# Ranks of the edges made in four blocks of columns, three of them during the scatter, and 14 turns of first gathers in place of 20

## The chip, the cores and the metric

The kernel is one program on one core of a Trainium2 chip. The metric is the device time of one execution in microseconds (us); lower is better. The engines are TensorE (PE, with its weight loads as PEld), VectorE (DVE), ScalarE (ACT), GpSimd (POOL) and SyncE (SP).

## The reference

Two graph layers over N = 6250 nodes of D = 256 features and E = 106250 edges, sorted by destination. Cut to what matters:

```python
h = (x - mean) * rsqrt(var + EPS) * gamma + beta            # statistics over the nodes
feat_in, feat_out = h @ W_in + b_in, h @ W_out + b_out
a_in  = segment_sum(feat_in[src]  * iw[:, None], dst, N)     # sum at the sorted end
a_out = segment_sum(feat_out[dst] * ow[:, None], src, N)     # sum at the unsorted end
xi, hh = concat(a_in, a_out) @ W_x2i + b_x2i, h @ W_h2h
x1 = layernorm(x + gates(xi, hh, h))
f  = (x1 - mean(x1)) / (std(x1) + 1e-4)
out = layernorm(x1 + segment_sum(iw[:, None] * f[src], dst, N) @ weight + bias)
```

## The kernel before

The edges stand in 208 groups of 512 (4 columns of 128; `CPG = 4`), and four groups are a turn (`RING = 4` buffers of gathered rows in `big`). POOL's program is a row of indirect DMAs, four to a group, each of 128 rows:

* **First gathers** (L541), groups 0 to 79: `FIRST = 20` turns. Rows x[src] come in; ACT scales them (`in_scale`, L665), DVE makes a one-hot matrix of the destinations (`hot_in`, L1518), PE multiplies (`in_mm`, L952), and DVE adds the product into `in_sums` (`add_in`, L1533). A gather of group g waits until `in_mm` of group g - 4 is done.
* **Scatter** (L547), all 208 groups in 52 turns: rows x[dst] are loaded as one block and spread by a one-hot product (DVE L1758, PE `out_mm` L1072), scaled by ACT (`out_messages`, L729) and written by an indirect DMA to slots of the table `messages`, so that the messages of one source tile stand together. Beside it DVE sums the weights (L1761, L1771, L1775, `add_weights` L1750) and once a turn helps with the tile's hidden rows (L1792, L1793, L1797).
* **Rest of the first gathers** (L541), groups 80 to 207 in 32 turns, with `back_mm`: the 232 pairs of message blocks are read back (SP, 260 KB a block), multiplied by one-hots (PE L1140) and added (DVE L1891). `pairs_of(g)` spreads the 232 pairs evenly over those groups, 1.81 to a group: one or two.
* The gates of the first layer, then the **second gathers** (L619), 208 groups, from the table of the first layer's result.

The slot of a message is its rank among the edges of its tile plus the tile's base. DVE makes the ranks during the first gathers. `rank_steps(k)` takes two of the 50 tiles at once (k and k + 25, packed in one number) over all 832 columns: compare, running sum, read the count (L1577), pick, add. There are 25 such k. The counts give the bases (`tile_bases` and what follows it). `base_steps(k)` then adds the bases, three instructions over 832 columns for each of 25 k (L1593 to L1595), in turns 14 to 18. `main_slots` turns ranks into slots: 16 columns before the scatter, the other 816 behind its first turn.

In the same turns x's statistics are made: 24 loads of 256 KB (`x_load`, two tiles of rows each, called a pair; four buffers `xs`) for the sums (PE L965, one pair a group, turns 1 to 6), and the same 24 again for the squares (DVE `x_shift` L1471, ACT `x_square` L660, PE L970, turns 7 to 13). Turns 14 to 19 prepare the weights.

`in_order` deals a list of steps out to the four groups of a turn, a run of consecutive steps to each. In `in_turn` one step stands between `hot_in(g)` and `add_in(g - 1)`, the others behind `add_in`. Every engine works in its program's order; semaphores join them.

Of the kernel before, what the change touches and what calls it, by code (L numbers as in the profile page):

```python
# [4 lines left out]
P = 128  # L5
# [20 lines left out]
FIRST = 20  # L26
# [55 lines left out]
def gnn_program(nc, x, src, dst, edge_weight, edge_weight_n2, gamma, beta, w_in, b_in, w_out, b_out,  # L82
                w_x2i, b_x2i, w_h2h, w_l1, b_l1, out):
    ctx = ExitStack()
    with ctx:
# [49 lines left out]
        win, mask, scan, rank, half_win, half_unit, upper_half, win_b = (part_c(k) for k in range(8))  # L135
        mask_i, scan_i = mask.bitcast(I32), scan.bitcast(I32)
        win_m, scan_m, rank_m, half_win_m, upper_m = (v[:, 0:NM] for v in (win, scan, rank, half_win, upper_half))
        mask_im, scan_im = mask_i[:, 0:NM], scan_i[:, 0:NM]
# [130 lines left out]
        unit, picked = banks23[:, 0:NM], banks67[:, 0:NM]  # L269
        numbers_in, numbers_out = banks67[:, NM:NM + P], ps[6][:, D + P:2 * D]  # L270
# [18 lines left out]
        RANKED = 14  # L289
        CLEARED = 2 * NTP // 5  # L290
        BASES_T = 5
# [9 lines left out]
        X_SHIFT = 1 + XPAIRS // RING  # L301
        PREP = RANKED
        BATCHES = -(-NT // RING)
        TURN_LAG, WEIGH_LAG, FINAL_LAG = 2, 3, 4

# [319 lines left out]
        def _(act):  # L625
# [59 lines left out]
            for i in range(X_SHIFT, X_SHIFT + XPAIRS // RING):  # L685
                for s in range(RING):
                    in_scale(i, s)
                    x_square(RING * (i - X_SHIFT) + s, s)
            x_square(XPAIRS, 0, TAIL, 1)
            scale_turn(X_SHIFT + XPAIRS // RING)  # L690
# [200 lines left out]
        def _(pe):  # L891
# [70 lines left out]
            def x_sum(i, s):  # L962

                pe.wait_ge(S[f"xs_loaded{s}"], 16 * i)
                nc.tensor.matmul(ps[0][:, :], ones[:, :], xs[:, s, :], start=isinstance(i, int) and i == 1 and s == 0, stop=False).then_inc(S["x_used"], 1)  # L965

            def x_square_sum(i, s):

                pe.wait_ge(S["x_sq"], RING * (i - X_SHIFT) + s - 1)
                nc.tensor.matmul(ps[1][:, :], ones[:, :], xs[:, (s - 2) % RING, :], start=isinstance(i, int) and i == X_SHIFT and s == 2,  # L970
                                 stop=False).then_inc(S["x_sq_used"], 1)

            def first_square_sums(i, s):
                if s >= 2:
                    x_square_sum(i, s)

            def last_square_sums(i, s):
                if s < 2:
                    x_square_sum(i, s)
                elif s == 2:  # L980
# [5 lines left out]
            for i in range(2, 1 + XPAIRS // RING):  # L986
                in_turn(i, x_sum)
# [121 lines left out]
            pe.wait_ge(S["base_chain"], 3 * PACKED + 1)  # L1109
# [170 lines left out]
        def _(dve):  # L1280
# [173 lines left out]
            V.memset(rank_m, 0.0)  # L1454
            link(V.tensor_scalar(upper_m, win_m, float(PACKED), None, ALU.is_ge))
            link(V.scalar_tensor_tensor(half_win_m, upper_m, -float(PACKED), win_m, ALU.mult, ALU.add))
            V.tensor_copy(numbers_in, iota[:, :])
            link(V.tensor_scalar(unit, upper_m, 4095.0, 1.0, ALU.mult, ALU.add))
# [6 lines left out]
            def x_shift(i, s):  # L1465

                def run():
                    dve.wait_ge(S[f"xs_loaded{s}"], 16 * (i - X_SHIFT + XPAIRS // RING + 1))
                    mean = mean_b[:, :].rearrange("p (o d) -> p o d", o=1).broadcast_to([P, 2, D])
                    v = xs[:, s, :].rearrange("p (t d) -> p t d", t=2)  # L1470
# [97 lines left out]
            def rank_steps(k):  # L1568

                def step(n, do):  # L1570
                    def run():
                        dve.wait_ge(S["rank_chain"], k * 5 + n + 1)
                        do().then_inc(S["rank_chain"], 1)
                    return run

                def pick():
                    V.tensor_scalar(cnt[:, bass.ds(k, 1)], picked[:, NM - 1:NM], rest_cnt[:, bass.ds(k, 1)], None, ALU.add).then_inc(S["rank_chain"], 1)  # L1577
                    dve.wait_ge(S["rank_chain"], k * 5 + 4)
                    return V.scalar_tensor_tensor(picked, half_win_m, iota_w[:, bass.ds(k, 1)], picked, ALU.is_equal, ALU.mult)
# [689 lines left out]
```

## Time and profile before

| | us |
|---|---|
| median of 3 runs | 3980.32 |
| lowest and highest | 3976.53, 3981.31 |
| the profiled execution's own time | 3986.79 |
| its span in the trace | 3985.0 |
| first gathers, groups 0 to 79 (first gather issued to first scatter issued) | 19.7 to 484.7 |
| scatter | 484.7 to 1736.2 |
| rest of the first gathers (first and last issue) | 1736.2 to 2520.7 |
| second gathers (first and last issue) | 2740.7 to 3946.9 |

The span runs from the first to the last instruction of the core. Busy time is that of each engine, PE's with modelled ends; the idle time before a group of instructions is put down to what seems to have ended it ("remote" is an event whose owner the trace does not know, "issue" is time of the engine's own sequencer).

### The profile page before, as it was taken

To read this page: it belongs to the slowest core of one execution; us is meant where nothing else is said; L and a number is where in the kernel's file an instruction comes from. 1 tells how busy PE (TensorE), PEld (TensorE's weight loads), DVE (VectorE), ACT (ScalarE), POOL (GpSimd) and SP (SyncE) were. 2 spreads that over 40 slices of the span, in tenths; PEclk is the share of its full clock that TensorE was granted. 3 is DMA by queue.
4 is the path that set the end of the run, shared out by engine and by line. 5 is a ranking of instruction groups with operands and counts; after the bars stand their busy time and mean duration, and the time that the engine had idled before them with its cause. 6 is when DMAs were issued, how large, how long until landed. Compare 5 with 4: busy or idle time off the path is not lost.

```text
span 3985.0 us, 48703 instructions
## 1 busy us (share of the span) xinstructions
PE 2654.7 (67%) x10701; PEld 1911.2 (48%) x10701; DVE 2213.6 (56%) x5022; ACT 1059.6 (27%) x3137; POOL 2560.1 (64%) x2706
## 2 busy tenths in 40 slices
PE   4665665665656565658888888995656555555467
PEld 3544533333333333337777777642434444434355
DVE  6866866655566655645565566684233333434244
ACT  3243332222222222234444444562000000000012
POOL 5666666666666666666666666576666666666653
PEclk8787887777877877779999999997777776677789
DMA  5443343333343433357877778554333333333333
GB/s 148 139 131 105 95 139 134 131 131 129 134 136 131 135 132 130 128 156 243 247 246 244 244 242 246 185 164 135 88 91 92 92 91 94 90 91 93 91 108 95
DMA packets 275048, 565.36 MB, mean 142 GB/s; under 512 B 55583, under 2 KB 121110, under 8 KB 274771
## 3 DMA queue, kind: packets, MB, share of 16 engines
q0 software_dynamic: 119808, 329.02, 26.5%
q1 hardware_dynamic: 146304, 223.88, 18.4%
q10 hardware_dynamic: 8660, 9.41, 0.7%
q8 instruction: 96, 1.57, 0.2%
q14 instruction: 180, 1.47, 0.1%
HBM read 419.19 MB, written 142.88 MB: 141 GB/s over the span
## 4 chain that ended last, share of the span: by engine, by line
PE 37%; another core or an unknown queue 22%; issue 17%; DVE 12%; POOL 5%; ACT 2%; SPq 2%; DMA 1%; DVEq 1%; ACTq 0%; POOLq 0%
PE ps L1140 10%; PE ps L952 9%; PE ps L1211 7%; POOL messages L547 4%; PE ps L1072 3%; DVE arena L1758 2%; PE ps L1173 1%; PE ps L1101 1%; ACT arena L729 1%; DVE arena L1761 1%; SPq L498 1%; PE ps L1258 1%; DVE arena L1771 1%; DVE ps L1582 1%
## 5 line engine op out<-in xcount | busy, mean ns | idle before, releaser
L547 POOL DMA_INDIRECT messages<-arena x832 | 825.8, 993 | 429.6 <-issue 243.7
L541 POOL DMA_INDIRECT arena<-in_x,arena x832 | 789.5, 949 | 473.4 <-issue 207.3
L619 POOL DMA_INDIRECT arena<-x_table,wh x832 | 801.4, 963 | 416.5 <-issue 238.4
L1211 PE MATMUL ps<-arena 128*128 x2048 | 624.4, 460 | 383.0 <-SPq L495 165.6
L1211 PEld LDWEIGHTS ps<-arena 128*128 128x128 f32 x2048 | 459.4, 232 | 550.4 <-issue 481.5
L952 PE MATMUL ps<-arena 128*128 128x128 f32 x3328 | 487.2, 308 | 245.8 <-issue 168.2
L952 PEld LDWEIGHTS ps<-arena 128*128 128x128 f32 x3328 | 457.5, 219 | 326.0 <-issue 283.3
L729 ACT ACTIVATE arena<-ps,arena 128x256 f32<-128x256 f32 x832 | 324.1, 480 | 901.3 <-remote 488.5
L2171 DVE TENSOR_TENSOR node_a<-node_a,ps 128x256 f32 x256 | 106.6, 417 | 746.4 <-remote 554.2
L1072 PE MATMUL ps<-arena 128*128 128x256 f32 x1664 | 481.0, 441 | 12.9 <-issue 7.4
L1072 PEld LDWEIGHTS ps<-arena 128*128 128x128 f32 x1664 | 374.6, 227 | 101.4 <-issue 40.1
L665 ACT ACTIVATE arena<-arena 128x256 f32<-128x256 f32 x832 | 352.0, 494 | 185.9 <-DMA arena<-in_x,arena 171.2
L1775 DVE TENSOR_REDUCE arena<-arena 128x128 f32<-128x512 f32 x208 | 214.8, 1033 | 193.6 <-remote 155.0
L2162 DVE TENSOR_SCALAR arena<-iota,arena 128x128 f32<-128x128 f32 x1024 | 291.6, 359 | 0.0
L1758 DVE TENSOR_SCALAR arena<-ps,pcol 128x512 f32<-128x512 f32 x208 | 154.4, 742 | 185.2 <-remote 177.1
L1891 DVE TENSOR_TENSOR node_c<-node_c,ps 128x258 f32 x464 | 195.3, 421 | 111.3 <-issue 72.4
L1140 PE MATMUL ps<-arena 128*128 128x258 f32 x928 | 224.4, 390 | 31.1 <-issue 30.8
L1061 PE MATMUL ps<-w,b_b 128*128 128x512 bf16 x208 | 93.6, 450 | 211.4 <-DVE arena L1758 154.8
L1140 PE MATMUL ps<-arena,bias_b 128*128 128x258 f32 x928 | 223.2, 389 | 15.7 <-issue 12.7
L1533 DVE TENSOR_TENSOR node_a<-node_a,ps 128x256 f32 x208 | 87.4, 420 | 259.4 <-remote 168.0
L872 ACT ACTIVATE arena<-ps 128x256 f32<-128x256 f32 x49 | 18.6, 383 | 762.0 <-PE ps L1249 662.5
L767 ACT ACTIVATE wh<-arena 128x2 f32 x464 | 94.9, 205 | 409.7 <-issue 267.1
(279 smaller groups left out, 3175.3 us busy)
## 6 DMA issues: line engine op xcount, KB each, us to landing
arena<-messages SPq DMA_DIRECT2D x464, 260.0 KB
arena<-in_x SPq DMA_DIRECT2D x304, 128.0 KB, 2.9
gate_rows<-arena SPq DMA_DIRECT2D x49, 384.0 KB
arena<-gate_rows SPq DMA_DIRECT2D x49, 384.0 KB, 3.0
arena<-in_x,arena POOLq DMA_INDIRECT x832
messages<-arena POOLq DMA_INDIRECT x832
arena<-x_table,wh POOLq DMA_INDIRECT x832
arena<-in_x SPq DMA_DIRECT2D x48, 256.0 KB
```

What stands on the lines that cost most here:

```text
L541: nc.gpsimd.indirect_dma_start(out=big[:, s, j, 0:D], out_offset=None, in_=x, in_offset=bass.IndirectOffsetOnAxis(ap=ids[:, j:j + 1], axis ...
L547: nc.gpsimd.indirect_dma_start(out=messages, out_offset=bass.IndirectOffsetOnAxis(ap=ids[:, j:j + 1], axis=0), in_=big[:, s, j, :], in_off ...
L619: nc.gpsimd.indirect_dma_start(out=last_rows[:, (g + 1) % LAST_ROWS, j * D:(j + 1) * D], out_offset=None, in_=x1_table, in_offset=bass.Ind ...
L665: last = nc.scalar.activation(big[:, s, j, 0:D], big[:, s, j, 0:D], ACT.Copy, scale=carried[:, bass.ds((RING * i + s) * CPG + j, 1), 1])
L729: last = nc.scalar.activation(big[:, s, j, 0:D], b[:, (j % 2) * D:(j % 2 + 1) * D], ACT.Copy, scale=carried[:, bass.ds(g * CPG + j, 1), 0])
L952: last = nc.tensor.matmul(ps[4 + h][:, k * P:(k + 1) * P], big[:, s, j, k * P:(k + 1) * P], hot[:, h, j, :], start=j == 0, stop=j == CPG - 1)
L1072: last = nc.tensor.matmul(b[:, (j % 2) * D:(j % 2 + 1) * D], hots[:, j * P:(j + 1) * P], tab[:, g % RING, :], start=True, stop=True)
L1140: last = nc.tensor.matmul(ps[2 * (k % 2) + u][:, 0:SUMS], hot_b[k][:, 2 * u + j, :], pair[:, k, 2 * u + j, 0:SUMS], start=j == 0, stop=j == 1)
L1211: last = nc.tensor.matmul(ps[g % LAST_SUMS][:, 0:D], last_hot[h][:, j, :], last_rows[:, bass.ds(k, 1), j * D:(j + 1) * D].rearrange("p o d ...
L1758: V.tensor_scalar(hot_flat(h) if hots is None else hots, spread[:, :], pcol[:, :], None, ALU.is_equal).then_inc(S["out_hot"], 1)
L1775: V.tensor_reduce(weighed[:, h, :], hot_w[:, h, :, :].rearrange("p j n -> p n j"), AX.X, ALU.add).then_inc(S["w_hot"], 1)
L2162: hot_j = V.tensor_scalar(last_hot[g % LAST_HOTS][:, j, :], iota[:, :], back[:, g * CPG + j:g * CPG + j + 1, 1], back[:, g * CPG + j:g * C ...
```

## The change

* `FIRST` is 14: groups 0 to 55 are gathered before the scatter, 56 to 207 behind it. `pairs_of` now spreads the 232 pairs over 152 groups.
* The counts of the 50 tiles are made first, by 50 single instructions over all 832 columns with an accumulated output (`count_step`), ten to a turn in turns 0 to 4.
* The ranks are made with the bases already known. The 832 columns are four blocks of 208 (`BLOCK_W`). For each block and each of 50 tiles `rank_steps(b, w)` has four instructions on 208 columns: compare, running sum that starts from the tile's running place, predicated copy of the sum into the rank, copy of the last sum as the new running place. Block 0 is made in turns 8 to 12, blocks 1, 2 and 3 during the scatter's turns 1 to 12, 13 to 25 and 26 to 38. `main_slots` follows each block.
* x's statistics take two pairs a group (`PER_GROUP = 2`): sums in turns 1 to 3, squares in turns 4 to 7.
* What unpacked and joined the packed ranks is gone.

```diff
-FIRST = 20
+FIRST = 14
+BLOCKS = 4
...
-        RANKED = 14
+        PER_GROUP = 2
+        RANKED = 8
...
+        def x_pairs(i, s):
+            return [PER_GROUP * (RING * i + s) + u for u in range(PER_GROUP)]
...
             def x_sum(i, s):
-                pe.wait_ge(S[f"xs_loaded{s}"], 16 * i)
-                nc.tensor.matmul(ps[0][:, :], ones[:, :], xs[:, s, :], ...).then_inc(S["x_used"], 1)
+                for q in x_pairs(i - 1, s):
+                    pe.wait_ge(S[f"xs_loaded{q % RING}"], 16 * (q // RING + 1))
+                    nc.tensor.matmul(ps[0][:, :], ones[:, :], xs[:, q % RING, :], ...).then_inc(S["x_used"], 1)
...
-            def rank_steps(k):
-                return [step(0, lambda: V.scalar_tensor_tensor(picked, half_win_m, iota_w[:, bass.ds(k, 1)], unit,
-                                                               ALU.is_equal, ALU.mult)),
-                        step(1, lambda: V.tensor_tensor_scan(picked, picked, zeros[...].broadcast_to([P, NM]), 0.0, ALU.add, ALU.max)),
-                        step(2, pick),
-                        step(4, lambda: V.tensor_tensor(rank_m, rank_m, picked, ALU.add))]
-            def base_steps(k):
-                return [step(0, lambda: V.tensor_scalar(picked, upper_m, delta[:, k:k + 1], basew[:, k:k + 1], ALU.mult, ALU.add)),
-                        step(1, lambda: V.scalar_tensor_tensor(picked, half_win_m, iota_w[:, k:k + 1], picked, ALU.is_equal, ALU.mult)),
-                        step(2, lambda: V.tensor_tensor(rank_m, rank_m, picked, ALU.add))]
+            def count_step(w):
+                    V.tensor_scalar(mask_m, win_m, iota_w[:, w:w + 1], 0.0, ALU.is_equal, ALU.add,
+                                    accum_out=cnt[:, w:w + 1]).then_inc(S["count_chain"], 1)
+            def rank_steps(b, w):
+                lo, hi = b * BLOCK_W, (b + 1) * BLOCK_W
+                return [step(0, lambda: V.tensor_scalar(member, win[:, lo:hi], iota_w[:, w:w + 1], None, ALU.is_equal)),
+                        step(1, lambda: V.tensor_tensor_scan(picked[b], member, zeros[...].broadcast_to([P, BLOCK_W]), run[:, w:w + 1],
+                                                             ALU.add, ALU.add)),
+                        step(2, lambda: V.copy_predicated(rank[:, lo:hi], member.bitcast(I32), picked[b])),
+                        step(3, lambda: V.tensor_copy(run[:, w:w + 1], picked[b][:, BLOCK_W - 1:BLOCK_W]))]
...
-            def out_turn(i, tiles, first=False):
+            def out_turn(i, tiles, first=False, beside=()):
                 for s in range(RING):
                     if not (isinstance(i, int) and i == 0 and s < 2):
                         out_hots(i, s)
+                    for step in beside[s::RING]:
+                        step()
                     if s == 2:
                         add_weights(i, 0)
                     elif s == 0 and not first:
                         add_weights(i - 1, 2)
...
-            main_slots(RING * CPG, NM)
-            for i in range(1, NT):
+            main_slots(RING * CPG, BLOCK_W)
+            for b in range(1, BLOCKS):
+                ranks = block_steps(b)
+                turns = range(max((b - 1) * BLOCK_T, 1), b * BLOCK_T)
+                a_turn = -(-len(ranks) // len(turns))
+                for n, i in enumerate(turns):
+                    out_turn(i, True, beside=in_order(ranks[n * a_turn:(n + 1) * a_turn]))
+                dve.wait_ge(S["rank_chain"], 4 * NTP * (b + 1))
+                main_slots(b * BLOCK_W, (b + 1) * BLOCK_W)
+            for i in range((BLOCKS - 1) * BLOCK_T, NT):
                 out_turn(i, True)
```

VectorE's program in a turn of the scatter, before: the first group of a turn from its second instruction on (L1761 to L1775), the two additions of weights (L1750), and the two instructions for the tile's hidden row.

```order
974 L1761 TENSOR_TENSOR arena<-ps,arena 128x512
975 L1765 COPY arena<-arena 128x4x4
976 L1771 TENSOR_TENSOR arena<-arena 128x512
977 L1775 TENSOR_REDUCE arena<-arena 128x128
978 L1524 TENSOR_LOAD low_two
979 L1750 REGISTER_ALU
980 L1750 ISA
981 L1750 TENSOR_TENSOR node_c<-node_c,ps 1x128
982 L1750 ISA
983 L1750 TENSOR_TENSOR node_c<-node_c,ps 1x128
984 L1792 TENSOR_TENSOR arena<-arena,scale_b 128x256
985 L1793 TENSOR_TENSOR arena<-arena,mean_b 128x256
```

The same place in the changed kernel, in a turn of block 1; lines 1598 to 1602 are the steps of `rank_steps`, and four of them stand here, one more before them, behind the reduction of the turn's first group.

```order
984 L1601 COPY_PREDICATED node_c<-node_c,ps 128x208
985 L1602 COPY alig<-ps 128x1
986 L1598 TENSOR_SCALAR node_c<-node_c,iota_w 128x208
987 L1599 SCALAR_TENSOR_TENSOR ps<-node_c,alig,zeros 128x208
988 L1532 TENSOR_LOAD low_two
989 L1747 REGISTER_ALU
990 L1747 ISA
991 L1747 TENSOR_TENSOR node_c<-node_c,ps 1x128
992 L1747 ISA
993 L1747 TENSOR_TENSOR node_c<-node_c,ps 1x128
994 L1791 TENSOR_TENSOR arena<-arena,scale_b 128x256
995 L1792 TENSOR_TENSOR arena<-arena,mean_b 128x256
```

Up to five steps now stand between a group's reduction and what follows it, and in the first group of a turn that is the addition of weights. In PE's program of the first gathers the sums of x stand two behind a group's product where one stood.

```order
15 L977 MATMUL ps<-arena,ones 128x512 x2
```

Its row before was this one:

```order
15 L965 MATMUL ps<-arena,ones 128x512
```

## Rows read from the trace of the kernel before

**Rows 1.** The page, section 1: busy us, share of the span, instructions

```profile
PE 2654.7 (67%) x10701; PEld 1911.2 (48%) x10701; DVE 2213.6 (56%) x5022; ACT 1059.6 (27%) x3137; POOL 2560.1 (64%) x2706
```

**Rows 2.** Windows of the four phases: length, engines' busy us (instructions), clock, DMA share, GB/s

```profile
20.00:484.00 464.00, 286.91 (x1439) 227.21 (x1440) 338.80 (x482) 157.03 (x358) 305.34 (x320) 0.80 0.43 123
485.00:1736.00 1251.00, 757.28 (x2392) 462.56 (x2390) 762.24 (x1411) 334.86 (x879) 825.57 (x832) 0.79 0.39 131
1737.00:2523.00 786.00, 673.56 (x3816) 584.02 (x3817) 464.48 (x1154) 370.56 (x1413) 483.02 (x512) 0.95 0.79 242
2741.00:3948.00 1207.00, 710.29 (x2326) 515.31 (x2327) 438.81 (x1476) 49.08 (x105) 801.06 (x832) 0.74 0.33 94
```

**Rows 3.** POOL's waits, 20 to 484 us: total us, times, longest

```profile
POOL arena L541 <- remote: 40.3, 19, 3.2
POOL arena L541 <- PE ps L952: 26.7, 12, 2.9
```

**Rows 4.** POOL's waits, 485 to 1736 us

```profile
POOL messages L547 <- ACT arena L729: 183.7, 46, 5.3
```

**Rows 5.** POOL's waits, 1737 to 2523 us

```profile
POOL arena L541 <- remote: 150.0, 107, 1.5
POOL arena L541 <- PE ps L952: 32.8, 17, 9.1
```

**Rows 6.** Windows within the first gathers, columns as in rows 2

```profile
66.00:206.00 140.00, 90.27 (x424) 69.14 (x425) 116.39 (x144) 38.01 (x89) 91.88 (x98) 0.79 0.46 136
206.00:366.00 160.00, 102.51 (x516) 78.70 (x515) 96.97 (x170) 63.44 (x143) 107.55 (x113) 0.81 0.43 125
366.00:484.00 118.00, 71.88 (x377) 60.53 (x378) 101.69 (x134) 38.00 (x90) 74.67 (x79) 0.80 0.33 95
```

**Rows 7.** VectorE by line and shape, 20 to 366 us: busy us, mean ns, idle before

```profile
L1582 DVE TENSOR_TENSOR_SCAN ps<-ps,zeros 128x832 f32<-128x832 f32 x25 | 47.3, 1892 | 0.2
...
L1579 DVE SCALAR_TENSOR_TENSOR ps<-node_c,iota_w,ps 128x832 f32<-128x832 f32 x25 | 27.3, 1090 | 0.9
...
L1584 DVE TENSOR_TENSOR node_c<-node_c,ps 128x832 f32<-128x832 f32 x25 | 25.4, 1015 | 0.2
...
L1577 DVE TENSOR_SCALAR cnt<-ps,rest_cnt 128x1 f32<-128x1 f32 x25 | 5.2, 209 | 0.2
```

**Rows 8.** VectorE by line and shape, 366 to 484 us

```profile
L1593 DVE TENSOR_SCALAR ps<-node_c,alig,basew 128x832 f32<-128x832 f32 x22 | 25.1, 1142 | 0.3
```

**Rows 9.** VectorE's timeline: one compare from SBUF to SBUF

```profile
31.38 0.53 DVE L1455 TENSOR_SCALAR node_c<-node_c 128x832 f32<-128x832 f32 x1
```

**Rows 10.** POOL's timeline in the rest of the first gathers, a group's first gathers

```profile
2052.81 0.94 POOL L541 DMA_INDIRECT arena<-in_x,arena  x1 [1.42 <-remote]
2054.06 0.94 POOL L541 DMA_INDIRECT arena<-in_x,arena  x1 [0.30 <-issue]
...
2058.80 0.94 POOL L541 DMA_INDIRECT arena<-in_x,arena  x1 [1.30 <-remote]
...
2064.91 0.94 POOL L541 DMA_INDIRECT arena<-in_x,arena  x1 [1.42 <-remote]
```

**Rows 11.** VectorE's timeline in one turn of the scatter

```profile
1016.37 0.75 DVE L1758 TENSOR_SCALAR arena<-ps,pcol 128x512 f32<-128x512 f32 x1 [2.96 <-remote]
...
1022.62 0.69 DVE L1797 TENSOR_TENSOR arena<-ps,bias_b 128x512 f32<-128x512 f32 x1 [1.54 <-PE ps L1101]
...
1024.60 0.74 DVE L1771 TENSOR_TENSOR arena<-arena 128x512 f32<-128x512 f32 x1
1025.37 1.04 DVE L1775 TENSOR_REDUCE arena<-arena 128x128 f32<-128x512 f32 x1
1026.33 0.74 DVE L1758 TENSOR_SCALAR arena<-ps,pcol 128x512 f32<-128x512 f32 x1
...
1032.34 1.02 DVE L1775 TENSOR_REDUCE arena<-arena 128x128 f32<-128x512 f32 x1 [3.94 <-remote]
```

**Rows 12.** The page, section 6: DMA issues, KB each, us to landing

```profile
arena<-in_x SPq DMA_DIRECT2D x304, 128.0 KB, 2.9
```

**Rows 13.** Windows of PE's products and pairs, 2000 to 2400 us: mean ns of one

```profile
L952 PE MATMUL ps<-arena 128*128 128x128 f32 x1052 | 140.1, 289 | 39.4 <-issue 39.2
L1140 PE MATMUL ps<-arena 128*128 128x258 f32 x480 | 114.5, 387 | 4.1 <-issue 4.0
```

More of the change, by code:

```diff
@@ L267, in gnn_program @@
         ps += [banks67[:, k * 2 * D:(k + 1) * 2 * D] for k in range(2)]
-        unit, picked = banks23[:, 0:NM], banks67[:, 0:NM]
-        numbers_in, numbers_out = banks67[:, NM:NM + P], ps[6][:, D + P:2 * D]
+        numbers_in, numbers_out = ps[7][:, D + P:2 * D], ps[6][:, D + P:2 * D]
+        picked = [ps[7 if b == 0 else 6][:, 0:BLOCK_W] for b in range(BLOCKS)]
+        assert BLOCK_W <= D + P and BLOCKS * BLOCK_T * RING == NG_PLAIN
         def tile_of(table, t, d=D):
@@ L985, in _ @@
             in_turn(1, x_sum)
-            for i in range(2, 1 + XPAIRS // RING):
+            for i in range(2, X_SHIFT):
                 in_turn(i, x_sum)
@@ L1597, in in_order, with block_steps @@
+            def block_steps(b):
+                return [step for w in range(NTP) for step in rank_steps(b, w)]
             def in_order(steps):
@@ L1708, in part_tiles @@
                 link(V.tensor_copy(part_wins[:, :], parts_f))
[L1710 removed]
+            beside = {X_SHIFT: counts[X_SHIFT * a_turn:], RANKED - 3: [counts_joined],
+                      RANKED - 2: [tile_bases, tile_ends, unit_ends, group_ends]}
             for i in range(X_SHIFT, RANKED - 1):
[L1712 to L1715 removed]
+                n = -(-len(beside[i]) // RING)
+                in_turn(i, in_order([step for s in range(RING) for step in
+                                     [x_shift(q) for q in x_pairs(i - X_SHIFT, s)] + (beside[i] + [lambda: None] * (n * RING))[s * n:(s + 1) * n]]))
             x_shift_last()
@@ L1719, in _ @@
             prep = {PREP: x_affine, PREP + 1: keep_affine, PREP + 2: add_biases, PREP + 4: lambda: scale_product(0), PREP + 5: lambda: scale_product(1)}
+            ranks = block_steps(0)
+            a_turn = -(-len(ranks) // (FIRST - 1 - RANKED))
             for i in range(RANKED, FIRST - 1):
-                in_turn(i, in_order([step for n in range(BASES_T) for step in base_steps((i - RANKED) * BASES_T + n)]), between=prep.get(i))
+                in_turn(i, in_order(ranks[(i - RANKED) * a_turn:(i - RANKED + 1) * a_turn]), between=prep.get(i))
             def turn_slots(link, a, r, m, h):
@@ L1799, in last_in_turn @@
             def last_in_turn():
-                left = [step for k in range((FIRST - 1 - RANKED) * BASES_T, PACKED) for step in base_steps(k)]
-                assert not left
                 g = RING * (FIRST - 1)
```

108 lines of the change are left out of this document (45 added, 63 removed).

## The prediction, made before the changed kernel was run

> **What bounds the kernel now.** I read the totals first. No engine is full over the span: POOL is busy 64% of it, VectorE 56% [rows 1]. So the windows of the phases come next. POOL's program is one row of 2496 indirect DMAs, and each phase lasts as long as POOL needs for its share. In the first gathers 320 take 464 us, 1.45 us each; in the scatter 832 take 1251 us, 1.50 us; in the rest of the first gathers 512 take 786 us, 1.54 us; in the second gathers 832 take 1207 us, 1.45 us [rows 2]. One gather is 0.94 us and 0.30 us of issue behind it, about 1.25 us [rows 10]. What is over that is waiting, and the waits of POOL say on what: in the first gathers 67 us, for products of PE [rows 3]; in the scatter 184 us in 46 waits, about one a turn, for the messages that ACT writes [rows 4]; in the rest of the first gathers 183 us in 124 waits, nearly one a group, for PE's product of four groups ago [rows 5]. So no phase is bound by POOL itself; each is a ring of engines that wait for one another, and the question is what the edit does to each ring.
>
> **Part 1: six turns move from the first phase to the third.** 96 gathers leave the first phase. What remains has 224. Its pace: in the stretch with the heavy rank steps 98 gathers take 140 us (1.43 us) with VectorE busy 83%; in the stretch with lighter VectorE work, 61%, 113 take 160 us (1.42 us); in that of the base steps, 86% busy, 79 take 118 us (1.49 us) [rows 6]. So lighter VectorE work brings little. What VectorE has to do there after the change: 25 packed ranks go, 1892 + twice 1090 + 1015 + 209 ns, 5.3 us each or 132 us, and 25 times three base steps at 1142, 1090 and 1015 ns, 81 us [rows 7, 8]. 50 counts come, each between 0.53 us (the compare of 832 columns, [rows 9]) and 1.09 us [rows 7], say 1.0 us, 50 us, and one block of ranks at 83 us (below). It is a smaller load for fewer turns, so I take 1.42 us for all: 224 x 1.42 = 318 us for 465 us, **-147 us** (bounds: -152 at 1.40, -140 at 1.45).
>
> The third phase gets the 96: 608 x 1.535 = 933 us for 786 us, **+147 us**. Will its pace hold? The pairs become thinner, 232 over 152 groups, 1.53 for 1.81. If PE's work set the pace that would help: PE is busy 674 of 786 us there [rows 2]. But a group with one pair passes hardly faster than one with two. The gathers shown are those of groups 131, 132 and 133, and they wait for the products of groups 127, 128 and 129 [rows 10]. By `pairs_of` group 127 has one pair and 128 has two, so one pair stands between the first two starts, 5.99 us apart, and two between the next, 6.11 us apart [rows 10]. The ring is product, `add_in`, next `hot_in`, next product, and the pairs fill its gaps. Groups with one pair grow from 0.19 to 0.47 of all. I grant 0.05 us a group, **-7 us** (bounds: +5; and -75, if the pace falls to the 1.42 us of the lighter first phase: 608 x 1.42 = 863 us).
>
> **Part 2: three blocks of ranks beside the scatter.** Per tile and block four instructions on 208 columns, none of which the trace shows. Between the copy of one column (209 ns) and 832 columns of the same kind: the compare lies between 0.21 and 0.53 us, 0.29 by the width; the running sum between 0.21 and 1.89, 0.63; the predicated copy between 0.21 and 1.02, 0.41; the copy 0.21 [rows 7, 9]. With 0.03 us between dependent instructions (L1771 to L1775, [rows 11]) that is 1.66 us for a tile, 83 us a block, 249 us for three, spread over 38 turns: 6.6 us a turn (7 in block 1, which has one turn less). A turn of the scatter is 24.06 us now (1251 us over 52), with VectorE busy 762 / 52 = 14.7 us [rows 2]. It would be busy 21.3 us.
>
> Where it lands decides. VectorE idles in a turn at three places: 2.96 us behind the second group, 1.54 us before L1797 behind the third, 3.94 us before the reduction of the first group of the next turn [rows 11]. One tile a group is dealt out behind each group's reduction. The 1.66 us behind the second and third group fall into idle time. The 1.66 us behind the last group delay the next L1758, for which PE's spreading and product wait; the 1.66 us behind the first group stand before `add_weights`, for which PE's transposes wait, and before L1758 of the second group, for which its product waits, and behind that ACT's messages and POOL. Bounds: nothing, if POOL's own wait of 4 us a turn (184 us / 46, [rows 4]) is from somewhere else and both are taken up; and 2 x 1.66 = 3.3 us a turn, 126 us, if neither is. I take 1.0 us a turn, nearer to nothing, since the two long idle times of a turn begin when PE's event is late and not VectorE's: **+38 us**.
>
> The Trainium skill, "VectorE: DVE Perf Modes", section on the TRN2 errata, states a fixed cost for each instruction, 58 cycles from SBUF and 120 from PSUM at 0.96 GHz, beside the columns; by that the four instructions would be an estimated 1.0 us and not 1.66, and the term 23 us and not 38. The trace has 0.21 us for a copy of one column from PSUM where the page's cost gives an estimated 0.13, so the rows' prices are used. The page's point, that many small instructions pay the fixed cost each time, speaks against cutting ranks into blocks, and the rows bear it out.
>
> **Part 3: the rest.** `main_slots` does the same columns in four pieces, about as long in sum: 0. x's statistics take two pairs a group. The same 48 loads come in 7 turns, and a load into one of four buffers can start only when PE has used it, now two groups before and not four. A load of 128 KB lands in 2.9 us [rows 12], one of 256 KB later. With 5.7 us a group there is room for it if PE's release is prompt: 0; at worst each of 24 groups waits one landing less what POOL's slack covers, about 1.5 us: +35 us. The unpacking steps that go (some ten instructions of about 1 us) lie beside gathers: 0.
>
> **Sum.** -147 + 147 - 7 + 38 = +31 us. The profiled execution took 3986.8 us (span 3985.0), 6.5 us over the median of 3980.3; on the median that is 4011, said as 4010 us.
>
> **Rivals.**
>
> * *The ranks fill idle time and the third phase gets faster.* What speaks for it: VectorE has 8 us idle in a scatter turn, and PE is busy 86% in the third phase, DMA engines 79% [rows 2]; both fall when the pairs are thinner. Against it: groups with one pair [rows 10]. Worked out at half of the bound: -35 us and the ranks at +5: 3950 us; at the full bound 3910. It decides if consecutive groups with one pair pass in under 5.9 us. Chance 0.27.
> * *The ranks lie fully on the scatter's chain.* Speaks for it: PE's rows wait for L1758 in each group, and the steps stand right in front of it twice a turn. Against it: POOL's wait begins elsewhere. 126 - 7 = +119: 4100 us. Chance 0.15.
> * *x's loads hold the first phase.* Two buffers a group, PE behind. +31 + 35: 4045 us. Chance 0.08.
> * *Everything cancels.* The lighter first phase runs at 1.38 us a gather and thinner pairs give 20 us: within 0.2%. Chance 0.08.
> * *A forecast as mine*, 3990 to 4035 us: 0.42.
>
> **How the numbers follow.** 0.2% is 8 us, about what a measurement of this kernel can tell from no change. Faster: 0.27 and a little from my own case, 0.29. Same: 0.08 and the edge of my case, 0.11. Slower: 0.60. The range 3935 to 4085 leaves out the far ends of both large rivals, about 2 in 10. My own case alone is 3990 to 4035.
>
> **What would show it.** Of the changed kernel: first scatter issued at about 338 us (19.7 + 318); the scatter's turns 1 to 38 at 25 us and 39 to 51 at 24 us; VectorE's four instructions at 1.66 us a tile; the rest of the first gathers 152 groups at 6.1 us. I am wrong if POOL's pitch in the third phase is under 1.50 us, if scatter turns with ranks are as long as those without, or if the first phase runs at POOL's own 1.25 us. The second gathers stay at 1207 us [rows 2]. The time in PE's share of the third phase is 289 ns for each half of a product and 387 ns for each half of a pair's [rows 13]; the changed kernel should show the same two means and more idle time before them.

## The result, and the profile after

The changed kernel takes 3991.29 us (median of 7 runs, 3982.26 to 4004.06), the kernel before, beside it on the same chip, 3978.97 us (7 runs, 3972.43 to 3981.77): ratio 1.0031, 95% interval 1.0020 to 1.0042, so **12.3 us slower**. The forecast was 31 us slower: the side was right, the size was not. (Ratios and intervals are those on record; the quotient of two printed medians differs from them by up to 0.0011.)

The profiled execution took 4004.06 us, the slowest of the seven, 17.3 us over the profiled one of before; its windows show where these 17 us are. First the page's section 1 of the changed kernel, then its windows of the four phases (columns as in [rows 2]).

```profile
PE 2682.8 (67%) x10701; PEld 1931.9 (48%) x10701; DVE 2351.9 (59%) x5729; ACT 1061.1 (27%) x3137; POOL 2574.7 (64%) x2706
```

```profile
20.00:354.00 334.00, 222.26 (x1057) 170.01 (x1058) 229.60 (x523) 118.48 (x264) 219.06 (x224) 0.79 0.46 133
355.00:1615.00 1260.00, 781.88 (x2390) 479.83 (x2388) 987.13 (x2029) 338.21 (x878) 830.24 (x832) 0.79 0.38 130
1616.00:2539.00 923.00, 748.48 (x4203) 656.38 (x4204) 487.94 (x1209) 409.54 (x1513) 575.30 (x608) 0.92 0.73 220
2758.00:3966.00 1208.00, 704.85 (x2328) 504.67 (x2329) 438.71 (x1477) 49.14 (x106) 804.68 (x832) 0.75 0.33 94
```

Read against [rows 2], with the exact starts of POOL's first DMA of each phase:

| phase | before | after | difference | forecast |
|---|---|---|---|---|
| first gathers | 465.1 us (20 turns) | 334.6 us (14 turns) | -130.5 | -147 |
| scatter | 1251.4 | 1260.5 | +9.1 | +38 |
| rest of the first gathers, up to the first second gather | 1004.5 | 1142.3 | +137.8 | +140 |
| second gathers | 1206.2 | 1207.8 | +1.6 | 0 |

With 0.2 us of later start that is +18.2 us, about the 17.3 us of the two profiled executions. These rows come from one execution of each kernel, 7.8 us above the median of before and 12.7 us above that of after, so a difference of a few us in a single row is not firm. VectorE's busy time in the scatter rose by 225 us (762 to 987), and the scatter grew by 9. Where it went is in VectorE's own groups: in the scatter of the changed kernel (busy, mean ns of one | idle before, releaser)

```profile
L1772 DVE TENSOR_REDUCE arena<-arena 128x128 f32<-128x512 f32 x207 | 213.9, 1033 | 130.1 <-remote 121.1 <-PE ps L1099 2.0 <-DVE arena L1768 1.3
L1755 DVE TENSOR_SCALAR arena<-ps,pcol 128x512 f32<-128x512 f32 x207 | 153.5, 742 | 36.6 <-remote 34.2 <-issue 2.1
...
L1599 DVE TENSOR_TENSOR_SCAN ps<-node_c,alig,zeros 128x208 f32<-128x208 f32 x150 | 98.9, 659 | 4.9
L1601 DVE COPY_PREDICATED node_c<-node_c,ps 128x208 f32<-128x208 int32 x150 | 58.1, 387 | 4.7
...
L1598 DVE TENSOR_SCALAR node_c<-node_c,iota_w 128x208 f32<-128x208 f32 x150 | 53.2, 354 | 1.4
...
L1602 DVE COPY alig<-ps 128x1 f32<-128x1 f32 x150 | 23.5, 157 | 4.6
```

The four rank instructions take 659 + 387 + 354 + 157 = 1557 ns a tile, 234 us for 150 tiles, and stand with next to no idle time before them (15.6 us in all, 0.10 us a tile). In the scatter POOL waits for ACT's messages about as long as before [rows 4], in a few more pieces:

```profile
POOL messages L557 <- ACT arena L740: 194.6, 56, 5.4
```

In the third phase POOL still waits in nearly every group, as in [rows 5]:

```profile
POOL arena L551 <- remote: 160.3, 121, 1.5
...
POOL arena L551 <- PE ps L963: 44.3, 27, 10.2
```

### The profile page after: what moved, and what is told of

Its sections match the earlier page's. It is cut to its first block, busy times and chain, and to the rows that moved or that the text cites. A ratio compares the mean times of both kernels' runs of the same rounds, so it can differ in the third digit from the quotient of the medians.

```text
span 4002.3 us, 49400 instructions
## 1 busy us (share of the span) xinstructions
PE 2682.8 (67%) x10701; PEld 1931.9 (48%) x10701; DVE 2351.9 (59%) x5729; ACT 1061.1 (27%) x3137; POOL 2574.7 (64%) x2706
## 3 DMA queue, kind: packets, MB, share of 16 engines
q14 instruction: 185, 1.52, 0.1%
## 4 chain that ended last, share of the span: by engine, by line
PE 29%; another core or an unknown queue 25%; DVE 24%; issue 15%; POOL 4%; DVEq 1%; ACT 1%; DMA 1%; ACTq 0%; SPq 0%; POOLq 0%
PE ps L1152 10%; PE ps L963 10%; DVE arena L1772 4%; DVE arena L1755 3%; PE ps L1223 3%; DVE arena L1758 2%; DVE ps L1599 2%; POOL messages L557 2%; DVE arena L1768 2%; POOL arena L551 2%; PE ps L1185 1%; DVE node_c L1601 1%; PE ps L1084 1%; DVE arena L2167 1%
## 5 line engine op out<-in xcount | busy, mean ns | idle before, releaser
L1223 PE MATMUL ps<-arena 128*128 x2048 | 615.8, 454 | 361.7 <-SPq L505 164.0
L1223 PEld LDWEIGHTS ps<-arena 128*128 128x128 f32 x2048 | 448.8, 228 | 538.3 <-issue 475.0
L963 PEld LDWEIGHTS ps<-arena 128*128 128x128 f32 x3328 | 465.1, 222 | 324.6 <-issue 306.3
L1084 PE MATMUL ps<-arena 128*128 128x256 f32 x1664 | 529.6, 476 | 7.0 <-issue 3.7
L1084 PEld LDWEIGHTS ps<-arena 128*128 128x128 f32 x1664 | 405.3, 245 | 95.8 <-issue 25.0
L1152 PEld LDWEIGHTS ps<-arena 128*128 128x128 f32 x928 | 179.4, 201 | 51.5 <-DVE arena L1883 18.0
```

What stands on the lines that cost most here:

```text
L963: last = nc.tensor.matmul(ps[4 + h][:, k * P:(k + 1) * P], big[:, s, j, k * P:(k + 1) * P], hot[:, h, j, :], start=j == 0, stop=j == CPG - 1)
L1084: last = nc.tensor.matmul(b[:, (j % 2) * D:(j % 2 + 1) * D], hots[:, j * P:(j + 1) * P], tab[:, g % RING, :], start=True, stop=True)
L1152: last = nc.tensor.matmul(ps[2 * (k % 2) + u][:, 0:SUMS], hot_b[k][:, 2 * u + j, :], pair[:, k, 2 * u + j, 0:SUMS], start=j == 0, stop=j == 1)
L1223: last = nc.tensor.matmul(ps[g % LAST_SUMS][:, 0:D], last_hot[h][:, j, :], last_rows[:, bass.ds(k, 1), j * D:(j + 1) * D].rearrange("p o d ...
```

## The experiments

The chips that ran them are of two kinds, and nothing here can be read without that. With the result and in one later set, **kind one**, the kernel before takes 3972 to 3985 us; in four other sets, each on another chip, **kind two**, it takes 3461 to 3482 us, the same program 12.7% shorter. The mean granted clock of an execution of the kernel before is about 0.82 on kind one and 0.88 to 0.89 on kind two. No chip of a known number stands in two sets, so whether the kind belongs to the chip or to its state at that time is not shown. Which kind a kernel ran on stands with it. Each kernel is compared with the kernel before on its own chip. All turns below are means of POOL's first scatter of turn 1 to that of turn 39 (38 turns with ranks) and from there to turn 52.

### The six turns and x's statistics put back (kind two)

```diff
-FIRST = 14
+FIRST = 20
-        PREP = RANKED
+        PREP = FIRST - 6
```

> The changed kernel with the first phase put back to 20 turns; ranks in four blocks, three beside the scatter, and x's statistics at two pairs a group stay. It isolates the six turns that moved. Theory 'the phases are worth the same' (a turn of first gathers costs about 23.4 us in the first phase and 24.1 us in the third): first phase 465 to 470 us for 335 us, third phase 24.1 x 6 = 145 us shorter, in sum 3 to 10 us faster than the changed kernel: 3981 to 3988 us. Rival 'thinner pairs gave something and thicker ones take it back': third phase less than 138 us shorter, sum 3990 us or more.

For the second kernel also:

```diff
-        PER_GROUP = 2
-        RANKED = 8
+        PER_GROUP = 1
+        RANKED = 14
...
```

> As the kernel with 20 turns of first gathers, and x's statistics again at one pair a group over 12 turns of loads; what is left of the change is the way in which ranks are made (counts, then four blocks, three beside the scatter). Theory 'x's loads held the first phase': the turns with squares take 22.5 us again and not 24.7 to 27.9, so 8 to 12 us faster than with two pairs a group, 3970 to 3978 us. Rival 'the shortfall of 17 us in the first phase is its last turns and block 0 of the ranks': within 3 us of the kernel with two pairs a group, 3981 to 3990 us.

Measured: 1.0173 (1.0159 to 1.0186) and 1.0177 (1.0163 to 1.0191) of the kernel before, 3537.2 and 3537.4 us for 3477.8 us. The absolute numbers of both expectations were for a chip of kind one and tell nothing. What can be read: two pairs a group cost nothing here that is clear of the intervals (some 5 us wide to either side). They do make VectorE wait. Its waits between 100 and 240 us, first with two pairs a group, then with one:

```profile
DVE arena L1479 <- DMA arena<-in_x: 28.9, 12, 7.0
DVE node_a L1541 <- PE ps L963: 15.9, 7, 3.1
```

```profile
DVE node_a L1541 <- PE ps L963: 73.9, 25, 5.7
DVE mean_b L1311 <- PE ps L1001: 4.6, 1, 4.6
```

The subtraction of the mean (L1479, the first instruction of the squares) waits 28.9 us for x's loads with two pairs and does not stand in the list with one; the first phase is 416.1 us against 410.9 us. Both were run twice more to see it on a chip of kind one, and came to kind two each time.

> The kernel with 20 turns of first gathers and x's statistics at two pairs a group, for the case that this set runs where the kernel before takes 3979 to 3984 us. There: a turn moved back costs 23.3 us in the first phase and gives back 24.1 us and a little thickening of pairs in the third; with the ranks' 9 us in the scatter and the 8 to 12 us of two late turns of squares left: +0.2 to +0.5% over the kernel before, 3988 to 4000 us. Where it takes 3475 us: 1.7% over it, as it did.

> As the last, with x's statistics at one pair a group. Theory 'x's loads held the first phase by 8 to 10 us in the place of record': 6 to 10 us less than the last run, first phase 463 to 468 us. Rival 'the late turns are made good by POOL later in the phase' (in the fast places the totals were equal, 3537.2 and 3537.4 us): within 3 us of the last run.

> The same with two pairs of x a group. Where the kernel before takes 3979 to 3984 us: 4 to 10 us more than with one pair a group, from two turns of squares at 26 to 28 us for 22 to 24 us; if nothing, POOL makes them good later in the phase. Where it takes 3475 us: 0 to 3 us more, as in two sets.

> 20 turns of first gathers, one pair of x a group; against the kernel before only the way of making ranks differs. Where the kernel before takes 3979 to 3984 us: 'longer of two things' gives 3 to 12 us more than the kernel before (the ranks' 9 us in the scatter and little else), 0.1 to 0.3%. The prediction's 1.0 us a turn would give 38 us, 0.95%. Where it takes 3475 us: 1.8% as before.

Measured: 1.0192 (1.0163 to 1.0221) and 1.0183 (1.0162 to 1.0205), then 1.0183 (1.0165 to 1.0201) and 1.0181 (1.0165 to 1.0197): no difference between their totals in three sets, though the first phase of the profiled execution was 4.7 to 5.2 us longer with two pairs in all three. The kernel with one pair differs from the kernel before only in how ranks are made, and that costs 1.8% there. It lies in the scatter, 1143.5 us for 1083.8.

### Where the rank steps stand in a turn (kind two)

`beside[s::RING]` behind group s becomes all steps behind the second and third group (shown), or all behind the last and first (`((0, 1), (), (), (2, 3))`):

```diff
-                    for step in beside[s::RING]:
+                    for step in [one for n in ((), (0, 1), (2, 3), ())[s] for one in beside[n::RING]]:
                         step()
```

> The changed kernel with all rank steps of a scatter turn dealt behind its second and third group, none behind the first and last. Theory 'idle time takes the ranks up wherever they stand, VectorE's total is what counts' (0.3 us a turn now): same as the changed kernel, 3987 to 3995 us. Rival 'where it lands decides' (only the steps behind the last and first group cost anything, and 3.1 us behind the second fits its 3 us of idle time): turns with ranks at 24.0 us like those without, 3979 to 3985 us. Third way: 3.1 us in one piece is too long for either place, the turns grow to 25.5 us or more, over 4030 us.

> The changed kernel with all rank steps of a scatter turn dealt behind its last and first group, none behind the second and third. Theory 'idle time takes the ranks up wherever they stand': same as the changed kernel, 3987 to 3995 us. Rival 'where it lands decides': the cost of these two places doubles or worse, turns with ranks at 24.8 to 27.5 us, 4005 to 4110 us.

Measured: 1.0139 (1.0123 to 1.0154) and 1.0167 (1.0154 to 1.0181); repeated:

> The changed kernel with the rank steps behind the second and third group only. Where the kernel before takes 3979 to 3984 us: 'longer of two things' has VectorE at 85% of a turn of 24.4 us and so no difference from the changed kernel (+0.2 to +0.45% over the kernel before); 'where it lands decides' has turns at 24.0 us, 0 to +0.15% over the kernel before.

> The changed kernel with the rank steps behind the last and first group only. Where the kernel before takes 3979 to 3984 us: 'longer of two things': no difference from the changed kernel (+0.2 to +0.45% over the kernel before); 'where it lands decides', the step of the prediction that put 1.0 us a turn on these two places: 24.8 us a turn or more, +0.5% or more.

> Rank steps behind the last and first group of a turn only, else the changed kernel. Where the kernel before takes 3979 to 3984 us: 'longer of two things' +0.2 to +0.45% over the kernel before, the same as the changed kernel; 'where it lands decides' +0.5% or more, turns with ranks at 24.8 us or more. Where it takes 3475 us: 1.7% as before.

1.0149 (1.0127 to 1.0170) and 1.0180 (1.0158 to 1.0202), then 1.0165 (1.0149 to 1.0180) for the last and first group. The changed kernel itself is at 1.0129. In turns: 22.38 us as changed, 22.56 and 22.54 with the steps behind the second and third group, 22.82, 22.72 and 22.70 behind the last and first. The dearest places cost 0.3 to 0.4 us a turn more than the even spread, and the idle places are no cheaper than it. Of the 1.6 us a turn that ranks cost on these chips, the place moves a quarter at most. But VectorE is full here, as the next section shows, and with a full engine the place can matter little by any theory. On kind one, where VectorE has room and for which the prediction was made, it was not tried. So "where it lands decides" is refuted for the full engine; for kind one only its size of 1.0 us a turn is, by the 0.27 us that the result shows.

### The changed kernel and the kernel before on kind two

> The changed kernel itself, beside the kernel before, since the first set ran where the kernel before takes 3478 us and not 3979. There the gathers go at POOL's own 1.25 us each and scatter turns with ranks took 22.6 us against 20.5 without. Theory 'the turn is the longer of two things, the ring through PE and ACT or VectorE's own sum': where the ring is short (kernel before near 3478 us) the ranks lengthen 38 turns by about 1.5 to 2 us each, 3530 to 3545 us, 1.5 to 2% slower; where the ring is long (kernel before near 3979 us) 0.2 to 0.4% slower as measured. Rival 'ranks cost the same everywhere': +12 us, 0.35% slower, in both.

> The kernel before itself, for a profile in the same place as the others of this set. Theory of the longer of two things: if it takes 3478 us, its scatter turns are all alike at 20.3 to 21.0 us and its gathers 20.0 to 20.8 us a turn in both phases; if 3979 us, 24.1 and 23.2 to 24.4 us as before.

Measured: 3515.43 us for 3472.38 us, ratio **1.0129** (1.0107 to 1.0151), in per cent four times the loss of the result; the kernel before against itself 1.0002 (0.9989 to 1.0016). The windows of the 38 turns (512 to 1427 and 380 to 1305 on the chip of the result; 458 to 1248 and 345 to 1195 here) in the kernel before and the changed one, first the chip of the result:

```profile
512.00:1427.00 915.00, 553.29 (x1751) 337.44 (x1750) 554.59 (x1031) 246.43 (x648) 603.82 (x609) 0.79 0.39 133
```

```profile
380.00:1305.00 925.00, 589.88 (x1756) 360.19 (x1755) 780.37 (x1644) 249.50 (x646) 609.56 (x608) 0.80 0.39 131
```

```profile
458.00:1248.00 790.00, 535.20 (x1767) 328.74 (x1765) 557.49 (x1035) 254.70 (x654) 604.68 (x609) 0.88 0.46 154
```

```profile
345.00:1195.00 850.00, 572.52 (x1753) 350.91 (x1752) 780.15 (x1643) 252.38 (x646) 616.05 (x609) 0.82 0.42 143
```

The third number of instructions and time is VectorE's. It does the same work on both kinds, 555 us before and 780 us after. On the chip of the result that is 61% and then 84% of a turn of 24.08 and 24.35 us; on kind two it is 71% and then **92%**, and the turn grows from 20.80 (where POOL's own 16 DMAs at 0.96 and 0.30 us already make 20.2) to 22.38 us. The expectation had 1.5 to 2%; it is less because the third phase gained, below.

### More of VectorE's work

In blocks and first phase alike, the running sum of each tile is done twice:

```diff
                         step(1, lambda: V.tensor_tensor_scan(picked[b], member, ...
+                        step(2, lambda: V.tensor_tensor_scan(picked[b], member, ...
```

> The changed kernel with the running sum of each tile and block done twice (the same result, 0.66 us more of VectorE per tile, 2.6 us a turn with ranks, 3 us in block 1). Theory of the longer of two things: VectorE is busy 23.5 us of a turn with ranks, and with its small unavoidable waits it is full; where the ring is short every added us is paid, 2.6 x 38 = 100 us over the changed kernel, less what the first phase hides, 90 to 130 us; where the ring is long (24.4 us a turn now) only what passes the ring, 25 to 25.5 us a turn, 20 to 50 us over the changed kernel. Rival 'idle time takes it up in proportion' (9 us for 225 us of ranks): 4 to 10 us over the changed kernel in either place.

> The changed kernel with each running sum done twice, once more, for the case that this set runs where the kernel before takes 3979 us: there the theory of the longer of two things gives 25 to 25.5 us a turn with ranks and 20 to 50 us over the changed kernel's 3991 us; where the kernel before takes 3475 us, 3645 to 3660 us as it did.

Measured on kind two 3651.87 us for 3472.38 us, 1.0526 (1.0505 to 1.0547), 136 us over the changed kernel, of which 108 us in the scatter and 27 us in the first phase. The expectation had 90 to 130 us over the changed kernel. The second set came to kind one: 4049.69 us for 3984.39 us, 1.0175 (1.0150 to 1.0200), 58 us over the changed kernel's 3991.29 of the other set, for 20 to 50 expected. Its profiled execution has a scatter of 1297.8 us, 37 us over the changed kernel, and a first phase 21 us longer. Its 38 turns, and those of the run on kind two:

```profile
400.00:1363.00 963.00, 607.32 (x1759) 368.98 (x1759) 881.39 (x1797) 252.67 (x648) 606.19 (x609) 0.78 0.37 126
```

```profile
371.00:1329.00 958.00, 602.07 (x1754) 367.83 (x1753) 877.04 (x1793) 252.89 (x647) 606.59 (x609) 0.79 0.37 127
```

This is the run that decides. The turn is 25.34 us on one kind and 25.21 us on the other, though without ranks they differ by 3.3 us, and VectorE is at 92% in both. So a turn is, to within 0.4 us, the longer of two things: what the ring of engines takes without ranks (24.08 or 20.80 us), and VectorE's sum divided by 0.92. The 0.92 is no law: it is what VectorE reaches in the runs where it is full, 90.5 to 92% of their turns. For the changed kernel the latter is 780 / 38 / 0.92 = 22.3 us: below 24.08 on the chip of the result, where the turn grew by only 0.27 us, and above 20.80 on kind two, where it became 22.38. The 0.27 us a turn, 10 us in 38 turns and so all of the scatter's +9.1, is what this reading leaves unexplained; it may be the place of the steps. The same work of ranks is nearly free on one chip and costs 1.6 us a turn on the other. The rival of the expectation, "idle time takes it up in proportion" (4 to 10 us over the changed kernel), is refuted on both.

### Two blocks in the first phase (kind two)

```diff
-            ranks = block_steps(0)
+            ranks = block_steps(0) + block_steps(1)
...
-            for b in range(1, BLOCKS):
+            for i in range(1, BLOCK_T):
+                out_turn(i, True)
+            for b in range(2, BLOCKS):
```

> The kernel with 20 turns of first gathers, with blocks 0 and 1 of the ranks both in the first phase (turns 8 to 18) and only blocks 2 and 3 beside the scatter (turns 13 to 38). Theory of the longer of two things: scatter turns 1 to 12 become as short as those without ranks; where the ring is short that is 12 x 1.8 = 20 to 26 us off the kernel with 20 turns (3511 to 3525 us), if the first phase takes the 78 us of block 1 at less than 1 us a turn; where the ring is long 0 to 5 us. Rival 'ranks cost their length wherever they stand': the first phase grows by what the scatter gives back, no difference.

Measured, with 20 turns of first gathers: 3518.32 us, 1.0135 (1.0112 to 1.0157), as expected some 0.4% better than the kernels with 20 turns and one block. Turns 1 to 12 went from 22.34 to 20.67 us, like those without ranks; turns 13 to 38, which keep their ranks, took 22.06 us for 22.36. The first phase grew by 7 us, 423.1 for 416.1, for 78 us of VectorE's work.

### A longer product in the scatter (kind one)

```diff
+                for j in (CPG - 2, CPG - 1):
+                    last = nc.tensor.matmul(ps[2 * h + j // 2][:, (j % 2) * D:(j % 2 + 1) * D], hots[:, j * P:(j + 1) * P],
+                                            tab[:, g % RING, :], start=True, stop=True)
                 last.then_inc(S["out_mm"], 1)
```

> The kernel before with the last two of the eight half products of each group of the scatter done twice, before PE's event for the group is given: about 0.9 us more of PE per group on every ring that passes through it, 3.6 us a turn, the same result. It makes the ring long where it is short, as the place in which the kernel before takes 3979 us has it. Both theories: the scatter's turns grow from 20.8 to between 22.5 and 24.4 us, the kernel by 90 to 190 us. It is the base for the next run.

> The changed kernel with the same two half products done twice in each group. Theory of the longer of two things (ring or VectorE's sum): with the ring at 23 to 24 us a turn the ranks lie in its idle time, so the scatter is 5 to 25 us longer than that of the kernel before with the same lengthening, where without it the difference is 58.6 us. Rival 'every us of ranks costs its share': the difference stays 45 to 65 us.

Meant for kind two, it ran on kind one. The edit repeats two of a group's four products, which is four of its eight halves; at 0.236 us a half (1.89 us for eight) that is the 0.9 us of the expectation. Measured: the kernel before so lengthened 4000.65 us for 3984.39, 1.0049 (1.0033 to 1.0066); the changed one 4008.78 us, 1.0066 (1.0049 to 1.0083); 8 us between them. The premise failed: 0.9 us more for each group should have been 3.6 us a turn, and the kernel before went from 24.08 to 24.38 us. Its window shows why PE's busy time is no measure of the ring here:

```profile
514.00:1440.00 926.00, 660.10 (x2370) 454.58 (x2369) 556.28 (x1031) 246.75 (x650) 601.12 (x608) 0.86 0.39 131
```

PE is busy 107 us more than in the same 38 turns of the kernel before, in 11 us more time, and its granted clock is 0.86 for 0.79. The run says that the ring of 24 us has slack at PE. It says nothing of the granted clock, since the work of PE rose with it; that is answered in the last section. With the product longer the scatters still differ by 8.6 us (1280.7 less 1272.1), as without (9.1), and the 38 turns by 0.31 us each (24.69 and 24.38). The profiled execution of the changed kernel, 4025.71 us, was the slowest of its four.

## Why the prediction was wrong

**The step that failed is the ranks beside the scatter, +38 us for 9 measured.** Its prices held: 1.56 us a tile and 0.10 us of gaps, 1.66 as forecast, and 249 us in the scatter. The Trainium skill, "VectorE: DVE Perf Modes", section on the TRN2 errata, gave by its fixed costs an estimated 1.0 us a tile; the rows of the changed kernel do not agree, with 1.56. The same section adds that its row for VectorE comes out too low for a single instruction. What failed is "where it lands decides": 1.0 us a turn was put on two places because PE waits behind them. The runs show in its place a balance over the whole turn. As long as VectorE's sum stays under 92% of the ring's turn, work put ahead of instructions that are waited for is made good within the turn but for some 0.3 us (0.27 in the result, 0.31 with the longer product); above 92% it is paid in full, wherever it stands to within 0.4 us. The ring on the chip of the result takes 24.08 us, and 22.3 us were needed. The reasoning "VectorE 14.7 us of 24.06, then 21.3" was in the text, with the right numbers; it should have been the price itself.

**The side was right with some luck.** The two large misses pulled opposite ways: the scatter cost 29 us less than forecast, and the first phase gave 16.5 us less. Had the first phase given its 147 us, the same scatter and third phase would have left the kernel some 4 us faster, which is no difference.

**The first phase, -147 us for 130.5.** Two things. The pace of 1.42 us was that of windows in mid-phase; 14 turns of the kernel before take 322.6 us and its last turn 26.4 us for 22.3, so at its own pace 14 turns come to about 327 us, not 318. That is 9 of the 17 us. The rest lies in turns 6 and 7, counted from 0, 26.1 and 27.9 us for 22.4 and 24.6 in the kernel before: VectorE's subtraction waits for x's loads, in the first phase of the changed kernel

```profile
L1479 DVE TENSOR_TENSOR arena<-arena,mean_b 128x512 f32<-128x512 f32 x24 | 16.5, 689 | 29.2 <-DMA arena<-in_x 24.5 <-issue 4.6
```

29 us in 4 turns, of which POOL's ring lets some 7 or 8 through. The rival "x's loads hold the first phase" had this mechanism, at 35 us and without the reader that waits. On kind two the same wait (28.9 us) cost 5 us of the first phase and nothing that shows in the total; that it costs 8 on the chip of the result is argued from turns, not shown by a run there.

**The third phase, +140 us for 137.8: right.** 608 gathers at 923 us are 1.52 each for the 1.535 less 7 us forecast; the median turn is 24.11 us for 24.38. The rival of thinner pairs was worth some 10 us here and not 35. Its bound is written as -75 us in the prediction; by its own product, 863 for 933 us, it is -70, which is the figure that the rival's times use.

On kind two this part goes another way. The third phase grew by only 91.5 us, since with the thinner pairs POOL never waits there and runs at its own 20.0 us a turn, for 20.7 before. Third phase of the kernel before, then of the changed one:

```profile
POOL arena L541 <- issue: 134.5, 440, 0.5
POOL arena L541 <- PE ps L952: 38.9, 57, 1.7
```

```profile
POOL arena L551 <- issue: 180.0, 591, 0.3
POOL arena L551 <- PE ps L963: 0.6, 2, 0.3
```

There the sum is -111.4 (first gathers), +58.6 (scatter), +91.5, +1.5: +40.2 us, 0.3 us of earlier start, and the rest behind the last second gather: spans 3512.8 and 3474.5 us, 38.3 apart. **The rest** (second gathers 1207.8 for 1206.2, `main_slots` in pieces) was nothing, as said.

Of the signs named ahead, these held: second gathers at 1207 us, 1.66 us a tile, the third phase not under 1.50 us a gather, pairs' halves at 385 to 388 ns for 387 and more idle time before the products (69.7 us for 39.4 between 2000 and 2400 us). These failed: the first scatter came at 354.5 us and not 338, turns with ranks took 24.35 us and not 25, next to 24.14 without ranks (turns 39 to 50), and the products' halves rose to 308 ns from 289 [rows 13], at a granted clock of 0.93 for 0.97 in those 400 us. No kernel tried here beats the kernel before on either kind.

## What to carry to other kernels

Work added to an engine in a ring is priced by comparing two sums over one period: that engine's busy time, divided by the 0.92 that it reaches when it is the bound, and the period of the ring without it. The excess is paid, and below it some 0.3 us of a turn of 24 stayed here; with the engine full, the place within the period moved a quarter of the price at most. Whether the place matters more with an engine that has room was not tried. A phase's own length, with its slow first and last turns, gives its pace, not a window from its middle. And a change that moves work into idle time should be timed on more than one chip, since the idle time may belong to the chip or to its state.

## What the runs showed of the hardware that was not expected

The same program took 3979 us on one kind of chip and 3473 us on the other. POOL's indirect DMAs take the same there, 0.94 to 0.95 us with 0.30 behind, and the other engines' instructions nearly so (VectorE 555 and 557 us in the 38 turns, a half of a product in the scatter 379 ns in the median). What differs is how long after the end of PE's records the next engine goes on. The third phase of the kernel before, POOL's timeline and PE's, on the chip of the result:

```profile
1971.02 0.95 POOL L541 DMA_INDIRECT arena<-in_x,arena  x1 [0.30 <-issue]
1973.41 0.94 POOL L541 DMA_INDIRECT arena<-in_x,arena  x1 [1.44 <-remote]
```

```profile
1968.55 1.95 PE L952 MATMUL ps<-arena 128*128 128x128 f32 x16
```

and on kind two:

```profile
1708.52 0.95 POOL L541 DMA_INDIRECT arena<-in_x,arena  x1 [0.30 <-issue]
1709.91 0.94 POOL L541 DMA_INDIRECT arena<-in_x,arena  x1 [0.45 <-PE ps L952]
```

```profile
1707.62 2.02 PE L952 MATMUL ps<-arena 128*128 128x128 f32 x16 [0.17 <-issue]
```

The product's records end at 1970.50 and the gather that waits starts 2.9 us later; on kind two they end at 1709.64 and it starts 0.27 us later. It is so in nearly every group (median 2.9 us, a tenth at 1.5 or less), and with it the gathers go at 6.1 us a group on one chip and at 5.2 on the other. In the scatter, ACT's first activation of a message begins a median 2.6 us behind the product's last record on the chip of the result, 0.04 us on kind two (turns 2 to 37, in the raw records). That is no fixed delay: in the kernel before on kind one, four groups in ten begin 0.04 us behind, half more than 2.5 us and a tenth more than 12 us. And it gives way as VectorE gets fuller: the median is 0.6 us in the changed kernel, and with each running sum done twice 96% of the groups begin 0.04 us behind. ACT's waits of this sort in the scatter of these three, on kind one (us in total, times, longest), tell the same:

```profile
ACT arena L729 <- remote: 488.5, 60, 15.8
```

```profile
ACT arena L740 <- remote: 416.9, 54, 13.9
```

```profile
ACT arena L741 <- remote: 142.9, 16, 13.9
```

So the ranks stand, in part, in time that late events left empty, which fits their low price there. A "remote" releaser in the waits of [rows 3] and [rows 5] is this: no record's end fits it, and on kind two the word doesn't occur in POOL's waits. The traces of kind one also hold only a third of the semaphore events of those of kind two (20431 for 63775 of the kernel before), so what ended a wait is told less surely there; the starts and ends of instructions do not hang on it. What holds PE's events back on kind one is open. Two causes are ruled out for the scatter. It isn't the low granted clock: on kind two the kernel with the running sums done twice has 0.79 in its 38 turns (row above), as on kind one, and the kernel with the steps behind the last and first group has 0.76, and in both the activation follows at 0.04 us.

```profile
337.00:1204.00 867.00, 582.41 (x1759) 363.04 (x1759) 784.45 (x1644) 253.48 (x647) 596.82 (x608) 0.76 0.42 140
```

Nor is it ACT's other wait, for the message rows of four groups before to be written: by the DMA packets of the kernel before on kind one, those have landed at least 3.3 us before the activation in each of these groups, a median 13 us. Whether the matmuls really run longer there than their modelled ends, or their events arrive late, these records can't tell.
